# Moving a router's first tiles into the attention before it, with bf16 ranks and marks, three-part weight loads and an earlier normalised input

## The chip, the cores and the metric

One core of one Trainium2 chip runs the whole kernel. The metric is the device time of one execution in microseconds, taken as the median of the runs shown. Engines are PE (TensorE, matmul; PEld is its weight load), DVE (VectorE), ACT (ScalarE), POOL (GpSimd) and SP, which here only issues DMAs.

## The reference

A post-norm vision tower of four blocks on 32 images of 37 tokens, width 256, 1184 tokens in all. The two stages that matter here are the mixture of experts of the third block and the attention stages before and after it.

```python
h = _layernorm(h + _L2_attn_ref(h, ...), axis=-1)
h = _layernorm(h + _L2_ffn_ref(h, ...), axis=-1)
h = _layernorm(h + _L3_attn_ref(h, ...), axis=-1)

def _L2_ffn_ref(x, router_kernel_DE, kernel_gating_EDF, kernel_up_EDF, kernel_down_EFD):
    logits_BSE = jnp.einsum('BSD,DE->BSE', x, router_kernel_DE)          # E = 8
    probs_BSE = jax.nn.softmax(logits_BSE, axis=-1)
    weights_BSK, indices_BSK = jax.lax.top_k(probs_BSE, 2)
    norm_weights_BSK = jax.nn.softmax(weights_BSK, axis=-1)
    ...
    gating = einsum(x, gating_EDF); act = silu(gating); up = einsum(x, up_EDF)
    down = einsum(act * up, down_EFD)                                    # D = 256, F = 512
    out_BSD = jnp.einsum('BSED,BSE->BSD', down, full_weights_BSE)
```

The attention after it starts with a layer norm of its own input (`_L3_attn_ref`: mean, variance, `rsqrt`, then two projections to 128 latents).

## The kernel before

**Tiles.** `X` holds the activations in SBUF as 11 tiles of 111 rows (three images each). Each stage is one block with a program per engine; between stages all semaphores are cleared and all engines meet at a barrier, so a stage starts when the slowest engine of the one before has ended. Each engine works through its own program in order. While a stage runs, SP loads the next stage's weights (`load_next`) into the other of two areas, `weights_even` and `weights_odd`.

**The attention before the experts** (`pair_attention`, stage L2) takes 16 pairs of images in 18 steps `s`. PE's program is written out by hand: in step `s` the scores of pair `s`, the transposes `p_T` of the probabilities of pair `s-1` in two halves, the transposes `o_T` of the output of pair `s-2`, one `o_project` every third step, and the `values` of pair `s-1`. Steps 16 and 17 have no scores any more. Step 16 holds `p_T(15)`, `o_T(14)`, `o_project(4)` and `values(15)`; step 17 holds `o_T(15)`, and then comes `o_project(5)`. DVE adds the residual and takes the statistics, POOL normalises into `X`. Tiles 0 to 7 of `X` are final after unit 3's norm.

**The experts** (`experts_ffn`, stage L2f). A preamble decides where each token goes. PE transposes all 11 tiles of `X` (22 transposes of 128 columns, L1600), ACT copies them to `XT` (L1616), PE multiplies by the 256x8 router (22 fp32 matmuls of 8 columns, L2434). DVE takes the softmax and the two best experts (L2313 to L2342). PE counts, with matmuls by a matrix of ones (L2441 to L2444, 12 matmuls in fp32), how many rows come before each row in each expert. From that DVE works out each row's slot among 27 slots (`NS`) of 128 rows, and builds `tiles`, `marks` (L2376 to L2381) and the one-hot matrices `place` (L2383, two instructions of 11x128 elements), all in fp32. PE multiplies place by marks (L2450, 22 fp32 matmuls of 54 columns): the result names for each slot position its source row and its gate. DVE turns it into `source`, `target` (integers) and `wslot`. One fp32 matmul shows as two records in the trace.

Then comes the loop over 27 slots. POOL gathers 128 rows of `expert_rows` by `source` (L2255, five gathers ahead), PE transposes them (L2459), multiplies by the gate and up weights of the slot's expert (L2464), transposes the product (L2484) and multiplies by the down weights (L2493). DVE scales the result by `wslot` (L2411), and POOL scatters it with an add into `expert_sums` (L2264); each scatter waits for the one before to have landed. SP's queue holds, in this order: `X` to `expert_rows`, the eight experts' weights (one DMA of 1536 KB each, rows of 12 KB, all counted on one semaphore), `X` to `expert_sums`, the next stage's weights, and, behind a wait for the last scatter, `expert_sums` back to `X` in three groups of 4, 4 and 3 tiles.

**The tail.** For each group DVE takes statistics (L1469, L1472), POOL makes `(var + eps) ** -0.5` (L1488, L1490), and DVE alone normalises all 11 tiles (L1480), after the statistics of all groups.

**The attention after the experts** (`latent_attention`, stage L3) starts with statistics of unit 0 (tiles 0 and 1) on DVE (L871), a power and the normalised input `xin` on POOL (L729 to L734), and only then PE's first transposes (L975).

Other stages end in a class `SplitNorm`, which the change uses here too: POOL makes scale and shift per group in three instructions, and both ACT (`on_act`) and DVE (`on_dve`) normalise tiles.

## Time and profile before

| what | value |
|---|---|
| median of 3 runs | 1169.78 us |
| the 3 runs | 1165.82, 1169.78, 1186.6 us |
| the profiled execution | 1169.65 us |
| its span in the trace | 1167.8 us |
| PE, PEld busy | 948.8 us (81%), 725.8 us (62%) |
| DVE, ACT, POOL busy | 584.6 us (50%), 486.1 us (42%), 329.1 us (28%) |
| mean granted clock of PE | 0.868 |
| moved by DMA | 46.53 MB |

The profiled execution lies 0.13 us from the median, and 1.85 us of it lie outside the trace's span. Times inside the trace are counted from the start of the span. A clock of 1.00 is 2.4 GHz and one of 0.50 is 1.2 GHz. The busy shares are means over nine stages.

### The profile page before, as it was taken

What the parts mean: (1) busy time and instruction counts of PE and PEld (TensorE: products, weight loads), DVE (VectorE), ACT (ScalarE), POOL (GpSimd) and SP (SyncE); (2) the same over time, 40 slices, a digit from 0 to 9 for tenths busy, and PEclk for the clock granted to TensorE, in tenths of its full rate; (3) what the DMA queues carried; (4) which work ended last, traced back from release to release, by engine and by line L of the source; (5) the groups of instructions that cost most, each with busy time, mean ns of one, the idle gap of its engine ahead of it and who ended that gap; (6) DMA issues with size and microseconds to landing.
All of it is one profiled execution on the core that took longest, in us unless ns stands there. A gap on an engine that the chain in (4) does not pass through costs nothing. (4 is left out here: it accounts for less than half of the span.)

```text
span 1167.8 us, 25327 instructions
## 1 busy us (share of the span) xinstructions
PE 948.8 (81%) x10056; PEld 725.8 (62%) x10056; DVE 584.6 (50%) x1264; ACT 486.1 (42%) x902; POOL 329.1 (28%) x426
## 2 busy tenths in 40 slices
PE   4899857499999799869975699999178999988564
PEld 4778625377777566658855466666066787777332
DVE  3466756456666289646644122222344456532475
ACT  3345557455555398634430122222013235432354
POOL 0211311534342000021330244443254454531101
PEclk9899968699999898889985699999677999985775
DMA  5200030200000100000009622222310000000001
GB/s 185 100 3 3 3 113 1 76 1 2 0 0 1 43 1 1 0 6 2 3 13 395 239 41 46 46 46 32 62 69 2 3 2 3 3 2 1 1 1 42
DMA packets 20538, 46.53 MB, mean 40 GB/s; under 512 B 4319, under 2 KB 14335, under 8 KB 18766
## 3 DMA queue, kind: packets, MB, share of 16 engines
q1 hardware_dynamic: 15246, 37.93, 9.1%
q0 software_dynamic: 5184, 7.08, 3.9%
q8 instruction: 78, 1.28, 0.5%
q14 instruction: 30, 0.25, 0.1%
HBM read 37.75 MB, written 7.25 MB: 39 GB/s over the span
## 5 line engine op out<-in xcount | busy, mean ns | idle before, releaser
L2464 PE MATMUL psum<-L2f_EW,weights_even 128*128 x216 | 102.8, 600 | 0.4 <-issue 0.4
L2418 DVE TENSOR_TENSOR weights_even<-psum,weights_even 128x512 f32<-128x512 f32 x27 | 18.7, 692 | 109.0 <-PE psum L2464 109.0
L2264 POOL DMA_INDIRECT expert_sums<-weights_even,L2f_target x27 | 42.8, 1584 | 94.1 <-DVE weights_even L2411 91.1
L996 PE MATMUL psum<-L_cT,weights_odd 128*128 128x222 f32 (+1 forms) x192 | 49.0, 389 | 9.2 <-DVE L_by_sin L884 8.0
L2464 PEld LDWEIGHTS psum<-L2f_EW,weights_even 128*128 128x128 f32 x216 | 37.5, 193 | 27.9 <-issue 27.9
L2286 ACT ACTIVATE weights_even<-psum 128x256 f32<-128x256 f32 x27 | 10.4, 384 | 106.8 <-PE psum L2459 74.3
L2152 PE MATMUL psum<-weights_even,L1f_H 128*111 128x256 f32 x176 | 46.7, 424 | 7.5 <-DVE L1f_H L2083 7.5
L2493 PEld LDWEIGHTS psum<-L2f_EW,weights_even 128*128 128x128 f32 x216 | 41.0, 190 | 17.6 <-issue 13.4
L2493 PE MATMUL psum<-L2f_EW,weights_even 128*128 x216 | 51.1, 379 | 0.8 <-ACT weights_even L2291 0.8
L884 DVE TENSOR_TENSOR L_by_cos<-psum,vectors_odd 128x444 f32<-128x444 f32 (+1 forms) x48 | 26.5, 553 | 48.7 <-PE psum L996 48.3
L823 ACT ACTIVATE L_PT<-psum 101x296 f32<-101x296 f32 x32 | 13.3, 417 | 83.2 <-PE psum L1037 82.6
L535 PE MATMUL psum<-L_xT,weights_odd 128*128 128x222 f32 (+1 forms) x192 | 43.9, 379 | 3.3 <-DVE L_V L467 1.9
L395 ACT ACTIVATE L_PT<-psum 101x296 f32<-101x296 f32 x64 | 27.0, 421 | 47.1 <-PE psum L585 47.1
L2152 PEld LDWEIGHTS psum<-weights_even,L1f_H 128*111 128x111 f32 x176 | 34.7, 199 | 18.5 <-DVE L1f_H L2083 8.9
L996 PEld LDWEIGHTS psum<-L_cT,weights_odd 128*128 128x128 f32 x192 | 35.5, 212 | 15.6 <-issue 13.4
L336 POOL TENSOR_TENSOR L_rs<-L_mv,ln_eps 111x2 f32<-111x2 f32 (+1 forms) x12 | 3.0, 254 | 142.9 <-DVE L_mv L482 135.9
L1069 PE MATMUL psum<-weights_odd,L_OT 128*111 128x256 f32 x176 | 41.2, 394 | 0.5 <-ACT L_OT L830 0.5
L2255 POOL DMA_INDIRECT weights_even<-expert_rows,L2f_source x27 | 26.9, 995 | 51.3 <-DVE L2f_source L2402 43.4
L535 PEld LDWEIGHTS psum<-L_xT,weights_odd 128*128 128x128 f32 x192 | 37.0, 213 | 5.2 <-ACT L_xT L364 4.2
L153 PE MATMUL psum<-L1a_W_high,L1a_xT_high 128*111 128x512 f32 x88 | 39.5, 449 | 0.9 <-DVE L1a_xT_low L1298 0.9
L748 POOL TENSOR_TENSOR L_P<-L_P,L_rc 101x592 f32<-101x592 f32 x16 | 19.2, 1200 | 70.5 <-DVE L_rc L902 70.5
L585 PE MATMUL psum<-ident,L_P 101*101 101x101 f32 x256 | 37.1, 268 | 1.8 <-ACT L_PT L395 0.8
(406 smaller groups left out, 2542.2 us busy)
## 6 DMA issues: line engine op xcount, KB each, us to landing
L2f_EW<-experts SPq DMA_DIRECT2D x8, 1536.0 KB, 18.9
weights_even<-L_w SPq DMA_DIRECT2D x4, 1024.0 KB
patch_ring<-patches SPq DMA_DIRECT2D x11, 333.0 KB, 3.3
weights_odd<-L_wqkv SPq DMA_DIRECT2D x2, 768.0 KB
out<-X SPq DMA_DIRECT2D x10, 111.0 KB
expert_rows<-X SPq DMA_DIRECT2D x1, 1056.0 KB, 5.3
expert_sums<-X SPq DMA_DIRECT2D x1, 1056.0 KB, 29.9
weights_odd<-L_wo SPq DMA_DIRECT2D x1, 1024.0 KB
```

The costliest lines, as they stand in the source:

```text
L153: mm = core.nc.tensor.matmul(out, left[a], right[b], start=first and n == 0, stop=last and n == len(passes) - 1)
L395: nc.scalar.activation(PT[:PR, s % 2, 4 * half:4 * half + 4].rearrange("p n (b q) -> p n b q", b=2), cols(core.bank(PTB)[:PR, 0:512], 4, 1 ...
L535: mm = nc.tensor.matmul(bank[:, c * NC2:c * NC2 + n], wqkv[:, kd, first + 128 * c:first + 128 * (c + 1)], xT[:, u % 2, kd, 0:n], start=kd ...
L585: mm = nc.tensor.transpose(core.bank(PTB)[:PR, 128 * i:128 * i + PR], P[:PR, s % 2, 2 * cq:2 * cq + 2].rearrange("p e k -> p (e k)")[:, 0: ...
L884: last = nc.vector.tensor_tensor(dst[:, i % 2, :, 0:k * T].rearrange("p h (i t) -> p h i t", i=k), src, w[table].unsqueeze(1).unsqueeze(1) ...
L996: mm = nc.tensor.matmul(bank[:, h * NC2:h * NC2 + width(u)], wu[:, (2 * g + h) * 128:(2 * g + h + 1) * 128], cT[:, u % 2, n // 4, 0:width( ...
L1069: mm = nc.tensor.matmul(core.bank(M2)[:R, m * D:(m + 1) * D], OT[:, c, first:first + R], wo[:, c, :], start=c == 0, stop=c == 7)
L2152: mm = nc.tensor.matmul(y_bank(t), H[:, c, t * R:(t + 1) * R], w2[:, c, :], start=False, stop=c == nf - 1 and (t % 2 == 1 or t == NT - 1))
L2255: nc.gpsimd.indirect_dma_start(xs[:, j % RING, :], None, rows[:, :], bass.IndirectOffsetOnAxis(ap=source[:, j:j + 1], axis=0)).then_inc(go ...
L2264: nc.gpsimd.indirect_dma_start(sums[:, :], bass.IndirectOffsetOnAxis(ap=target[:, j:j + 1], axis=0), Y[:, j % 2, :], None, compute_op=ALU. ...
L2464: mm = nc.tensor.matmul(core.bank(bank), xsT[:, j % 2, c, :], EW[:, expert[j], first + c * NF:first + (c + 1) * NF], start=c == 0, stop=c ...
L2493: mm = nc.tensor.matmul(core.bank(5)[:, 0:D], HT[:, (j - 1) % 2, c * 128:(c + 1) * 128], EW[:, expert[j - 1], 2 * KD * NF + c * D:2 * KD * ...
```

## The change

- **Router.** The transposes, copies and logits of tiles 0 to 7 (`ROUTED = 8`) move into `pair_attention`: 16 transposes at the start of PE's step 16, 4 ACT copies behind `p_T(15, 1)`, the logits of tiles 0 to 3 at the end of PE's step 16 and those of tiles 4 to 7 at the end of step 17, ahead of `o_project(5)`. The experts' stage keeps tiles 8 to 10.
- **Ranks and marks in bf16.** `ones`, `sooner`, `both`, `place`, `tiles` and `marks` are bf16. The row number goes in two parts that bf16 holds exactly; the gates are no longer in `marks` but go, split in three bf16 parts (`g_parts`, five small DVE instructions ahead of the wait for `mark_ps`), through 22 further matmuls (`gate_marks`) after the sources. `place` is built in four instructions instead of two, `marks` in two instead of four.
- **Weights in three loads.** For each expert, gate, up and down weights are loaded by DMAs of their own (24 of 512 KB, rows of 4 KB), gates of all experts first, with three semaphores. The next stage's weights are issued only after the second slot's result.
- **Tail.** `SplitNorm` with groups of 2, 4 and 5 tiles; ACT normalises tiles 2 to 5, 9 and 10, DVE 0, 1 and 6 to 8. POOL computes one spare power before the tail. A class `Lead` makes the next attention's `xin` of unit 0 there: DVE statistics, POOL power, DVE scaling. `latent_attention` starts with unit 1 on DVE and POOL, and PE transposes unit 0 at once.

```diff
@@ pair_attention
+                    if route and s == NP:
+                        for b in range(ROUTED // 2):
+                            act.wait_ge(rt_ps, b + 1)
+                            bank = core.bank(M1 if b == 3 else S0 + b)
+                            nc.scalar.activation(route.XT[...], bank[...], ACT.Copy).then_inc(rt_done, 1)
...
+                def routed_T():
+                    pe.wait_ge(shifted, NP)
+                    pe.wait_ge(v_done, v_phases(NU, 0))
+                    pe.wait_ge(norm_done, ROUTED // 2)
+                    for b in range(ROUTED // 2):
+                        for m in range(2):
+                            for c in range(KD):
+                                mm = nc.tensor.transpose(bank[...], X[:R, 2 * b + m, c * 128:(c + 1) * 128], core.ident[:R, :R])
+                        mm.then_inc(rt_ps, 1)
+                def routed_logits(first, last):
+                    pe.wait_ge(rt_done, last // 2)
+                    pe.wait_ge(next_sem, 16 * len(next_loads))
+                    for t in range(first, last):
+                        router_logits(core, route.XT, route.router, t)
...
+                    if route and s == NP:
+                        routed_T()
                     if 1 <= s <= NP:
                         p_T(s - 1, 0)
...
                     if 1 <= s <= NP:
                         values(s - 1)
+                    if route and s == NP:
+                        routed_logits(0, ROUTED // 2)
+                if route:
+                    routed_logits(ROUTED // 2, ROUTED)
                 o_project(NU - 1)
@@ experts_ffn, SP
-                for e in range(NEX):
-                    sp.dma_start(EW[:, e, :], core.dram["experts"][e]).then_inc(w_in, 16)
+                for n, sem in enumerate((gates_in, ups_in, downs_in)):
+                    for e in range(NEX):
+                        part = slice(n * KD * NF, (n + 1) * KD * NF)
+                        sp.dma_start(EW[:, e, part], core.dram["experts"][e][:, part]).then_inc(sem, 16)
...
+                sp.wait_ge(y_done, 2)
                 load_next(sp, next_loads, next_sem)
@@ experts_ffn, POOL
-                tail.pool(pool)
+                nc.gpsimd.tensor_tensor(spare[:], core.eps[:], core.nhalf[:, 0:1], ALU.pow)
+                tail.on_pool(pool, 0)
+                pool.wait_ge(lead_var, 1)
+                nc.gpsimd.tensor_tensor(lead.rs[:R], lead.mv[:R, :, 1], core.eps[:R].broadcast_to([R, 2]), ALU.add)
+                pool.drain()
+                nc.gpsimd.tensor_tensor(lead.rs[:R], lead.rs[:R], core.nhalf[:R, 0:2], ALU.pow).then_inc(lead_rstd, 1)
+                tail.on_pool(pool, 1)
+                tail.on_pool(pool, 2)
@@ experts_ffn, ACT
+                tail.on_act(act, 1)
+                tail.on_act(act, 2, 9, 2)
@@ experts_ffn, DVE
-                    V.tensor_tensor(marks[:R, u, :, 0, :], tiles[:R, u], w["row_ids"]..., ALU.mult)
-                    V.tensor_tensor(marks[:R, u, :, 1, :], tiles[:R, u], g2..., ALU.mult)
-                    V.tensor_tensor(place[:R, u], ids..., inside..., ALU.is_equal).then_inc(marked, 1)
+                    V.tensor_tensor(marks[:R, u], tiles[:R, u].unsqueeze(2)..., rows_b[:R].unsqueeze(3)..., ALU.mult)
+                    for p in HALVES:
+                        V.tensor_tensor(place[:R, u, p], ids_b..., inside_b[:R, u, p]..., ALU.is_equal).then_inc(marked, 1)
...
+                V.tensor_copy(g_parts[:R, :, :, 0], g_u)
+                dve.drain()
+                V.tensor_tensor(g_rest[:R, :, :, 0], g_u, g_parts[:R, :, :, 0], ALU.subtract)
...
+                V.tensor_copy(g_parts[:R, :, :, 2], g_rest[:R, :, :, 1])
...
+                for u in range(2):
+                    V.tensor_tensor(gate_marks[:R, u], tiles..., g_parts..., ALU.mult).then_inc(gates_marked, 1)
+                dve.wait_ge(gate_ps, 1)
...
-                for g in range(len(GROUPS)):
+                for g in range(2):
                     dve.wait_ge(back[g], 32)
                     tail.stats(g)
-                for g in range(len(GROUPS)):
-                    tail.norm(dve, g)
+                tail.on_dve(dve, 0)
+                dve.drain()
+                for m in range(2):
+                    V.bn_stats(lead.stat[:R, m], X[:R, m, :])
+                dve.drain()
+                for m in range(2):
+                    last = V.bn_aggr(lead.mv[:R, m], lead.stat[:R, m])
+                last.then_inc(lead_var, 1)
+                dve.wait_ge(back[2], 32)
+                tail.stats(2)
+                dve.wait_ge(lead_rstd, 1)
+                for m in range(2):
+                    V.tensor_scalar(lead.xin[:R, m], X[:R, m, :], lead.mv[:R, m, 0:1], lead.rs[:R, m:m + 1], ALU.subtract, ALU.mult)
+                tail.on_dve(dve, 2, 6, 3)
@@ latent_attention
-                stage(0)
+                stage(1)
                 nc.gpsimd.memset(P[:, :, :, T:64], 0.0).then_inc(zeroed, 1)
-                stage(1)
...
-                input_stats(0)
                 input_stats(1)
...
-                    pe.wait_ge(x_staged, u + 1)
+                    after(pe, x_staged, u)
```

## Rows read from the trace of the kernel before

**Rows 1.** Stretches of one execution: us, each engine's busy time, PE clock, DMA
```profile
607.00:611.00 4.00, 0.00 (x0) 0.00 (x0) 0.79 (x3) 0.00 (x0) 2.79 (x4) 0.50 0.00 0
...
611.10:623.60 12.50, 12.34 (x66) 12.27 (x66) 0.17 (x2) 2.97 (x6) 0.00 (x0) 0.50 0.93 311
...
660.30:821.80 161.50, 159.85 (x594) 97.92 (x594) 31.33 (x54) 41.09 (x82) 62.98 (x48) 0.99 0.26 40
```

**Rows 2.** Timeline, last steps of the attention, PE
```profile
598.62 0.60 PE L585 MATMUL psum<-ident,L_P 101*101 101x101 f32 x4
...
602.11 0.77 PE L598 MATMUL psum<-L_V,L_PT 101*37 101x34 f32 x32
...
604.76 0.39 PE L607 MATMUL psum<-ident,L_O 101*128 101x101 f32 x2 [1.89 <-DVE L_O L455]
...
605.60 1.12 PE L618 MATMUL psum<-weights_odd,L_OT 128*111 128x256 f32 x4 [0.45 <-ACT L_OT L401]
```

**Rows 3.** Timeline, an earlier attention step, four transposes of X
```profile
549.57 0.54 PE L527 MATMUL psum<-ident,X 111*128 111x111 f32 x4
```

**Rows 4.** Timeline, router, ranks and marks in the experts' preamble
```profile
611.12 4.30 PE L1600 MATMUL psum<-ident,X 111*128 111x111 f32 x22 [4.40 <-SPq L126]
...
612.13 0.54 ACT L1616 ACTIVATE weights_even<-psum 128x444 f32<-128x444 f32 x1 [6.58 <-PE psum L1600]
...
615.22 8.25 PE L2434 MATMUL psum<-weights_even 128*111 128x8 f32 x44
...
630.03 3.81 PE L2444 MATMUL psum<-L2f_both,L2f_ones 111*111 111x80 f32 x20
...
638.25 0.84 DVE L2376 TENSOR_TENSOR L2f_slot_tile<-vectors_even,L2f_which 111x297 f32<-111x297 f32 x2
...
640.68 3.15 DVE L2383 TENSOR_TENSOR weights_even<-vectors_even,L2f_inside 111x1408 f32<-111x1408 f32 x2
...
642.35 9.63 PE L2450 MATMUL psum<-L2f_marks,weights_even 111*128 111x54 f32 x44 [8.52 <-DVE weights_even L2383]
...
652.68 0.18 DVE L2402 CAST L2f_source<-L2f_owner 128x27 uint32<-128x27 f32 x1
```

**Rows 5.** Timeline, first gather, first wide work and first scatter of the slots
```profile
653.77 1.30 POOL L2255 DMA_INDIRECT weights_even<-expert_rows,L2f_source  x1 [43.43 <-DVE L2f_source L2402]
...
660.32 0.66 PE L2459 MATMUL psum<-ident,weights_even 128*128 128x128 f32 x2 [8.33 <-DMA weights_even<-expert_rows,L2f_source]
...
671.33 1.89 PE L2493 MATMUL psum<-L2f_EW,weights_even 128*128 x8
...
674.58 1.64 POOL L2264 DMA_INDIRECT expert_sums<-weights_even,L2f_target  x1 [13.24 <-DVE weights_even L2411]
```

**Rows 6.** Issues of the experts' weights, then DMA totals of 627:640 and 652:656
```profile
612.18 8.42 SPq L2239 DMA_DIRECT2D L2f_EW<-experts  x8
...
DMA packets 510, 5.55 MB, mean 427 GB/s; under 512 B 59, under 2 KB 59, under 8 KB 59
...
DMA packets 440, 1.48 MB, mean 370 GB/s; under 512 B 44, under 2 KB 105, under 8 KB 429
```

**Rows 7.** Timeline, experts' tail and start of the next attention
```profile
827.66 2.75 SPq L2246 DMA_DIRECT2D X<-expert_sums  x6
...
831.97 1.41 DVE L1469 BATCH_NORM_STATS2 L2f_stat<-X 111x6 f32<-111x256 f32 x4 [9.75 <-DMA X<-expert_sums]
...
838.70 1.05 POOL L1490 TENSOR_TENSOR L2f_rs<-L2f_rs,minus_half 111x4 f32<-111x4 f32 x1 [4.58 <-issue]
...
839.78 3.80 DVE L1480 TENSOR_SCALAR X<-X,L2f_mv,L2f_rs 111x256 f32<-111x256 f32 x11 [2.00 <-POOL L2f_rs L1490]
...
849.54 0.97 PE L975 MATMUL psum<-ident,L_xin 111*128 111x111 f32 x4 [27.84 <-POOL L_xin L734]
```

**Rows 8.** Timeline, bf16 transposes in the last stage, PE at half clock
```profile
1100.64 0.93 PE L2678 MATMUL psum<-identb,L3f_XQ 111*128 111x111 bf16 x8 [3.23 <-DVE L3f_XQ L2581]
```

**Rows 9.** A stretch of the next attention
```profile
880.00:893.60 13.60, 12.87 (x185) 9.93 (x185) 6.01 (x10) 3.12 (x6) 8.53 (x13) 0.50 0.01 3
```

More of the change, by code:

```diff
@@ L1497, with router_logits, __init__ @@
 AHEAD, AHEAD_L3 = 8, 10
+ROUTED = 8
+LOGITS = 3
+def router_logits(core, XT, router, t):
+    for c in range(KD):
+        mm = core.nc.tensor.matmul(core.bank(LOGITS)[:R, t * 8:(t + 1) * 8], XT[:, c, t * R:(t + 1) * R], router[:, c, :],
+                                   start=c == 0, stop=c == KD - 1)
+    return mm
+class Route:
+    def __init__(self, core, w):
+        self.router = cols(w["L2_router"], KD, 8)
+        self.XT = cols(core.areas[0][:, KD * 8:KD * 8 + KD * TOK], KD, TOK)
+class Lead:
+    def __init__(self, stack, core):
+        sb = lambda n, s, d=F32: stack.enter_context(core.nc.sbuf_tensor(f"lead_{n}", s, d))
+        self.xin = cols(core.areas[0][:, 5888:6400], 2, D)
+        self.stat, self.mv, self.rs = sb("stat", [128, 2, 6]), sb("mv", [128, 2, 2]), sb("rs", [128, 2])
 class Int8Weights:
@@ L2203, in experts_ffn @@
         Y = cols(area[:, at + 6 * NF:at + 6 * NF + 2 * D], 2, D)
[L2204 to L2206 removed]
+        assert at + 6 * NF + 2 * D + KD * NEX <= 5888
+        tiles = sb("slot_tile", [128, 2, NT, NS], BF16)
+        marks, gate_marks = sb("marks", [128, 2, NT, 2, NS], BF16), sb("gate_marks", [128, 2, NT, 3, NS], BF16)
+        ones, sooner = sb("ones", [128, R], BF16), sb("sooner", [128, R], BF16)
+        ids_b, rows_b = sb("ids_b", [128, 128], BF16), sb("rows_b", [128, NT, 2], BF16)
+        which_b, inside_b = sb("which_b", [128, 2, NT], BF16), sb("inside_b", [128, 2, NT], BF16)
+        g_parts, g_rest = sb("g_parts", [128, 2, NT, 3], BF16), sb("g_rest", [128, 2, NT, 2])
+        spare = sb("spare", [128, 1])
         lg, pr = sb("logits", [128, NT, NEX]), sb("probs", [128, NT, NEX])
@@ new lines, in _ @@
+                for u in range(2):
+                    V.tensor_tensor(gate_marks[:R, u], tiles[:R, u].unsqueeze(2).broadcast_to([R, NT, 3, NS]),
+                                    g_parts[:R, u].unsqueeze(3).broadcast_to([R, NT, 3, NS]), ALU.mult).then_inc(gates_marked, 1)
+                dve.wait_ge(gate_ps, 1)
+                found = core.bank(5)[:, 0:3 * NS]
+                V.tensor_copy(wslot[:], found[:, 0:NS])
+                for p in range(1, 3):
+                    dve.drain()
+                    V.tensor_tensor(wslot[:], wslot[:], found[:, p * NS:(p + 1) * NS], ALU.add)
@@ L2441, in _ @@
                 nc.tensor.matmul(core.bank(2)[:R, 0:NT * NEX], ones[:R, :R], flat, start=True, stop=True)
-                nc.tensor.matmul(core.bank(1)[:R, 0:NT * NEX], w["sooner"], flat, start=True, stop=False)
+                nc.tensor.matmul(core.bank(1)[:R, 0:NT * NEX], sooner[:R], flat, start=True, stop=False)
                 for d in range(1, NT):
@@ L2755, in tower @@
         run[2](2)
-    for n in range(3, 7):
+    prepared["route"] = Route(core, w[6])
+    for n in range(3, 6):
         run[n](n)
     with ExitStack() as stack:
+        prepared["lead"] = Lead(stack, core)
+        run[6](6)
         prepared["glu"] = GluWeights(stack, nc, w[8])
```

142 lines of the change are left out of this document (89 added, 53 removed).

## The prediction

> **What bounds the kernel now.** I read the stretches first, then the timeline of the stages that the diff touches. The stretches show three kinds of time around the experts. In the loop over the slots PE is busy 159.9 of 161.5 us at full clock [rows 1]; the diff changes nothing there, so the loop's length stays. Ahead of it lies a preamble of 49.2 us, from PE's first transpose at 611.12 to the first slot's transpose at 660.32 [rows 4, 5], in which PE and DVE take turns and PE runs at 0.50: it fell there by 607, behind the attention's thin end, and 12.5 us of transposes and 8-column matmuls did not raise it [rows 1]. Behind it lies a tail of DMA, POOL and DVE in which PE waits 27.84 us [rows 7]. The change shortens preamble and tail and pays in the attention. The sum is therefore made of the chain of single events, not of busy shares.
>
> **The attention's end.** Three pieces go into PE's in-order program. (a) 16 transposes stand ahead of p_T(15), which began at 598.62, just when its input was there. Four such transposes took 0.54 us at full clock, the last one's end included [rows 3], so about 0.11 each: 1.8 us, with the waits ahead of them long met; I take 2.0, which moves every later step. (b) The logits of tiles 0 to 3, 8 matmuls. All 22 took 8.25 us at half clock [rows 4], 0.375 each, so 3.0 us at half and 1.5 at full clock. They stand behind values(15), which ended at 602.88; PE then waited 1.89 us for DVE [rows 2]. At full clock they fit into that wait and cost nothing; the copies they need (0.54 us each [rows 4]) are ready, since ACT has nothing else there but two o_T and p_T copies, and o_project(4) gives it 2 us. At half clock they cost 1.1. (c) The logits of tiles 4 to 7 stand between o_T(15) and o_project(5), where PE had 0.45 us to spare [rows 2]: 1.5 - 0.45 = 1.05 at full clock, 2.55 at half. Which clock? It had fallen by 607, in the thin stretch behind values(15) [rows 1, 2]. Everything there moves by 2.0, and I let the fall move with it, to 609, when (c) is done; so I take full clock and add 0.25 for a slower o_project(5). Sum **+3.3 us**; ends +2.8 and +6.8 (all at half clock, with 1.12 us of o_project doubled). POOL and DVE have no new work here.
>
> **The preamble.** All prices are at half clock, which also ruled there before.
> - Router: 3 tiles are left. PE ended the logits at 623.47. Now 4 transposes (4.30 / 22 = 0.195 each [rows 4], 0.8), a copy (0.54 and some 0.3 of waits) and 6 matmuls of 0.375 (2.25) end at 3.9 us behind the start instead of 12.35. **-8.45**. DVE's new casts hide behind this.
> - Ranks: 12 fp32 matmuls; ten of them took 3.81 us, so 4.6. The nearest bf16 row at half clock is 8 transposes in 0.93, 0.116 each [rows 8]: 1.4. **-3.2**; ends -3.6 (0.08 each) and -1.8 (0.23 each, one fp32 record).
> - Marks: before, PE started its 22 matmuls at 642.35 and ended at 651.98, 8.15 us behind DVE's last place instruction at 643.83; source was written at 652.86 [rows 4]. In bf16 DVE writes the same elements; two more instructions for place and two fewer for marks cancel, and one more cast adds 0.1. DVE's instruction rate stays (the same operation took 1.575 us for 1408 elements [rows 4]); PE's 22 matmuls by 0.116 run beside it, and the last five end at about 644.7. But DVE's program is now the bound: expert ids (1.35), then five small instructions for the gates at an estimated 0.25 each, drain included, then three for the source: 643.9 + 1.35 + 1.25 + 0.7 = 647.2. **-5.65**; if bf16 halved DVE's element time, for which no row speaks, 2.7 more would go. The gates' own 22 matmuls and DVE's products of 891 elements (about 1 us each) take some 4.5 us after that, hidden by the first gather's 6.5 us. Cover gone, they cost up to 1 us.
>
> On DVE, the Trainium skill (VectorE: DVE Perf Modes) says that a two-source operation gets its double rate if every tensor is 16-bit with step 1 or -1; here the second source is broadcast with step 0, so no gain. No row here shows such an operation. With the double rate the result would be 1148.3.
>
> - First gather: it took 6.5 us from issue to PE's transpose, with the queues full of weights [rows 5]. The queues are full in the new place too, so I keep 6.5. It would be at worst the whole backlog, at best 3 us less.
>
> So the first slot starts 17.3 us sooner after the stage's start: 49.2 becomes 31.9.
>
> **The weights.** 12.58 MB in rows of 4 KB instead of 12. With 12 KB rows the queue moved 427 GB/s, with mostly 4 KB rows 370 [rows 6]. By 12.5 us, 3.9 MB had moved, 1.25 of it expert_rows [rows 1]; with the rest and 0.65 MB of gathers 10.6 MB remain, 28.6 us at 370: down weights at 41.1 us behind the start. The first matmul by them, at 671.33 before [rows 5], now stands at 42.9. It fits, by 1.8 us; gates and ups, each a third, come well before their use. expert_sums (1.25 MB) is written by 45, the first scatter (674.58 before) needs it at 46.1. SP issues 24 instead of 8 (8.42 us [rows 6], so up to 25): it stays ahead of the data. Cost **0**; at 311 GB/s [rows 1] 3.7 us of stall. The next stage's 2.9 MB now wait for y_done 2 and move beside the first slots: nothing stands behind them in SP's queue before the last scatter, gathers are five slots ahead, and a scatter may be late by some 5 us before DVE's second buffer waits. Cost 0.
>
> The Trainium skill speaks against the split: DMA: Bandwidth & Descriptors, section Bandwidth, asks for at least 1 MiB per DMA and gives 341 GB/s at 1 MB; these have 0.5 MB. At that rate the down weights stall PE for about 0.7 us, 1151.7 in all. No row here has loads of that size alone.
>
> **The tail.** Before: loads issued at 827.66, statistics from 831.97, POOL's power only at 838.70 behind 4.58 us in which it waited for nothing shown, DVE's 11 tiles from 839.78 to 843.58 [rows 7]. Now the spare power takes that pause while the loads fly. Two tiles are in at 830.9; DVE's statistics end at 832.2; POOL's scale of two at 833.8 (estimated 1.5); DVE's next four at 835.2, its two tiles and the lead's statistics at 837.1; the lead's power at 838.3; POOL's groups of four and five at 840.3 and 842.5 (2.0 and 2.2: power 1.05 [rows 7], two small ones, two drains); the last tiles on ACT and DVE at 843.8. So the stage ends 0.2 later, and POOL, not DVE, sets it. But PE now starts the next attention by transposing, instead of at 849.54, 5 us behind that stage's start at 844.5: **-4.7** with the 0.2. Unit 1's statistics and scaling on DVE and POOL lie beside unit 0's projections. Ends -6 and -1.7.
>
> **Sum.** 1169.65 + 3.3 - 8.45 - 3.2 - 5.65 - 4.7 = 1150.95, with the 1.85 us outside the span unchanged. The median is 0.13 above the profiled time: **1151**, 1.6% faster. Its own range is 1147 to 1156.
>
> **Rivals.**
> 1. *Weights bound the start.* At 311 GB/s the down weights come 3.7 us late: 1155. For it: the slack is 1.8 us of 42.9. Against: 370 was measured with small packets among them. 0.16.
> 2. *The spare power doesn't take the pause*, the change not doing what it says: the 4.58 us come again behind the loads, of which about 3 reach the end: 1154. For it: no row says what the pause is. 0.08.
> 3. *The attention's end at half clock*, +6.8: 1154.5. For it: 12.5 us of such transposes and logits left the clock at 0.50 [rows 1], so they may not hold it at 1.00 either. 0.10.
> 4. *The next attention keeps its clock.* It ran at 0.50 for 13.6 us with PE busy 12.9 [rows 9]. Nothing in the change aims at that, but everything there moves by 19 us; if it stays at 1.00, some 5.5 us fall away: 1145.5. The opposite, a new fall elsewhere, is as possible and costs the same: 1156.5. 0.14 and 0.06.
> 5. *Slower than before.* If DMAs of 4 KB rows fall below 216 GB/s, the 10.6 MB take over 49 us and PE's stall exceeds the 18.7 us gained; at 200 GB/s it is 22.6: 1174. Against: every stretch with weights moved 311 or more. 0.03.
>
> **Chances.** Forecast 0.43, the rest as given. 2% is about what a measurement of this kernel tells from no change; it lies at 1146.4. Rival 4's better half (0.14) and the far lower edge of the forecast (0.06) lie below: 0.2. Slower by over 2%: 0.01. Within: 0.79. The range of 8 in 10 is 1143 to 1160.
>
> **What will show it.** In the new trace: p_T(15) 2 us behind values(14), o_project(5) about 3 us later than before; lg_ps 4 us behind the stage's start; ten and more bf16 matmuls at about 0.12 us in ranks and marks; first slot 32 us behind the start; no DMA wait at the first down matmul; POOL's power in the tail without a pause; PE in the next attention within 1 us of its start. Wrong would make it a gather that waits for the whole backlog, a clock different from the one before in the attention's end or the slots' first steps, or a longer POOL chain in the tail.

## The result, and the profile after

| what | before | after |
|---|---|---|
| median | 1170.28 us (4 runs, 1165.82 to 1186.6) | 1149.6 us (4 runs, 1145.2 to 1154.38) |
| the profiled execution, its span | 1169.65, 1167.8 us | 1149.84, 1148.0 us |
| mean granted clock of PE | 0.868 | 0.874 |

The ratio is 0.9845, 95% interval 0.9811 to 0.9878: 1.5% faster, and within the 2% that a measurement of this kernel tells from no change. Some executions of the same kernel run about 2% longer at a lower granted clock; the ratios leave them out (the medians don't), and of the two profiles further on that are of such executions, those with eight loads and with paced loads, only the stretches at the experts are read.

The whole span is no good ruler for terms of 2 us, so I cut it at single events of PE's program. The chain that the change touches runs from the start of values(14), the last work ahead of the moved transposes, to PE's first transpose in the next attention: 252.10 us before (597.44 to 849.54), 235.36 after (596.62 to 831.98), 16.74 less. The span fell by 19.80; 3.06 of that lie outside of the chain.

| piece of the chain, us | before | after | difference | forecast |
|---|---|---|---|---|
| values(14) to p_T(15) | 1.18 | 2.56 | +1.38 | +2.0 |
| p_T(15) to the stage's start (SP's first issue) | 12.54 | 14.77 | +2.23 | +1.3 |
| start to logits done | 12.42 | 4.08 | -8.34 | -8.45 |
| `both` written to the ranks read | 4.74 | 1.37 | -3.37 | -3.2 |
| ranks read to the instruction that writes `source` | 18.81 | 13.04 | -5.77 | -5.65 |
| softmax and top two, and `source` to PE's first slot transpose | 13.19 | 13.56 | +0.37 | 0 |
| that transpose to the last scatter | 163.52 | 163.46 | -0.06 | 0 |
| last scatter to the next attention's first transpose | 25.70 | 22.52 | -3.18 | -4.7 |
| sum | 252.10 | 235.36 | -16.74 | -18.7 |

Each piece runs between the starts of two instructions; only the one of `both` begins where its writing ends.

The attention's end, PE's timeline (start, length, line, output and inputs, tile, count, idle time before it and its releaser) and one ACT row, to be held against [rows 2]:

```profile
597.60 1.74 PE L638 MATMUL psum<-ident,X 111*128 111x111 f32 x16
599.18 0.52 PE L593 MATMUL psum<-ident,L_P 101*101 101x101 f32 x4
...
601.22 1.83 ACT L430 ACTIVATE weights_even<-psum 128x444 f32<-128x444 f32 x4
602.53 0.77 PE L606 MATMUL psum<-L_V,L_PT 101*37 101x34 f32 x32
...
603.23 1.73 PE L1536 MATMUL psum<-weights_even 128*111 128x8 f32 x16
...
605.19 0.39 PE L615 MATMUL psum<-ident,L_O 101*128 101x101 f32 x2 [0.23 <-DVE L_O L463]
605.42 2.19 PE L1536 MATMUL psum<-weights_even 128*111 128x8 f32 x16
...
607.47 2.03 PE L626 MATMUL psum<-weights_odd,L_OT 128*111 128x256 f32 x4
```

Two stretches of the same place (length, then busy time of PE, PEld, DVE, ACT and POOL, and behind them the granted clock, DMA share and GB/s):

```profile
606.00:607.00 1.00, 1.00 (x9) 1.00 (x8) 0.00 (x0) 0.00 (x0) 1.00 (x1) 0.67 0.00 0
607.00:608.00 1.00, 1.00 (x5) 0.89 (x5) 0.00 (x0) 0.00 (x0) 1.00 (x2) 0.50 0.00 0
```

The first eight logits matmuls (16 records) fill the pause ahead of o_T(15), which shrank from 1.89 to 0.23 and comes 6.01 behind p_T(15) where it came 6.14 behind it: they cost nothing. The second eight push o_project(5) from 6.98 to 8.29 behind p_T(15), and the clock falls to 0.50 while they run (0.67 on average in the first of the two stretches), so that o_project(5) takes 2.03 instead of 1.12.

The preamble, the answer to [rows 4, 5] (PE, DVE and POOL rows of its timeline):

```profile
613.98 1.34 PE L2554 MATMUL psum<-ident,X 111*128 111x111 f32 x6 [4.49 <-PEq L126]
615.59 2.41 PE L1536 MATMUL psum<-weights_even 128*111 128x8 f32 x12 [0.26 <-ACT weights_even L2355]
...
623.84 1.07 PE L2567 MATMUL psum<-L2f_both,L2f_ones 111*111 111x80 bf16 x10
...
629.60 0.85 DVE L2464 TENSOR_TENSOR L2f_slot_tile<-L2f_ids_b,L2f_which_b 111x297 bf16<-111x297 bf16 x2
...
631.22 1.69 DVE L2472 TENSOR_TENSOR weights_even<-L2f_ids_b,L2f_inside_b 111x768 bf16<-111x768 bf16 x2
...
635.25 0.41 PE L2574 MATMUL psum<-L2f_marks,weights_even 111*128 111x54 bf16 x5 [0.28 <-DVE weights_even L2472]
...
637.99 0.18 DVE L2501 TENSOR_SCALAR L2f_source<-L2f_mark 128x27 uint32<-128x27 f32 x1
...
639.09 1.66 POOL L2323 DMA_INDIRECT weights_even<-expert_rows,L2f_source  x1 [25.97 <-DVE L2f_source L2501]
...
639.63 1.93 PE L2580 MATMUL psum<-L2f_gate_marks,weights_even 111*128 111x81 bf16 x22 [3.97 <-DVE L2f_gate_marks L2506]
...
646.00 0.66 PE L2589 MATMUL psum<-ident,weights_even 128*128 128x128 f32 x2 [4.43 <-DMA weights_even<-expert_rows,L2f_source]
...
656.98 1.89 PE L2627 MATMUL psum<-L2f_EW,weights_even 128*128 x8
```

The marks' matmuls end 2.3 us ahead of `source`: DVE's own order is the bound. The gates' 22 matmuls are over at 641.56, while the first gather is still under way: PE waits 4.43 us for it. The first down matmul has no wait. Two stretches show DMA with loads of 0.5 MB:

```profile
626.00:640.00 14.00, 2.09 (x28) 1.51 (x29) 12.01 (x38) 0.00 (x0) 0.91 (x1) 0.50 1.03 412
640.00:650.00 10.00, 4.79 (x27) 2.61 (x25) 1.12 (x4) 2.05 (x3) 5.50 (x6) 0.50 1.03 398
```

The tail, which answers to [rows 7]:

```profile
809.46 1.55 POOL L2332 DMA_INDIRECT expert_sums<-weights_even,L2f_target  x1 [2.95 <-DMA expert_sums<-weights_even,L2f_target]
810.46 1.16 POOL L2341 TENSOR_TENSOR L2f_spare<-ln_eps,minus_half 128x1 f32<-128x1 f32 x1
813.18 2.75 SPq L2314 DMA_DIRECT2D X<-expert_sums  x6
...
817.36 0.19 POOL L1743 TENSOR_TENSOR L2f_rs<-L2f_mv,ln_eps 111x2 f32<-111x2 f32 x1 [5.74 <-DVE L2f_minus_mean L1736]
...
822.13 0.70 POOL L1745 TENSOR_TENSOR L2f_rs<-L2f_rs,minus_half 111x2 f32<-111x2 f32 x1 [4.58 <-issue]
...
823.21 0.74 DVE L1763 TENSOR_SCALAR X<-X,L2f_mv,L2f_rs 111x256 f32<-111x256 f32 x2 [2.02 <-POOL L2f_norm_shift L1747]
...
827.93 3.06 ACT L1755 ACTIVATE X<-X,L2f_norm_shift,L2f_rs 111x256 f32<-111x256 f32 x6 [22.71 <-POOL L2f_norm_shift L1747]
...
831.93 0.35 SPq L131 DMA_DIRECT2D weights_even<-L_wg  x1
...
831.98 0.97 PE L1005 MATMUL psum<-ident,weights_even 111*128 111x111 f32 x4 [24.62 <-PEq L126]
```

The spare power ran at once, and the pause of 4.58 us, to the hundredth the one of [rows 7], stands again between POOL's first small addition and its first power. Between these two instructions the program has one thing: the first `pool.drain()` since the indirect DMAs.

### The profile page after: what moved, and what is told of

Same layout as the page of the kernel before. It is cut to its first block and busy times, and to the rows that moved or that the text cites. A ratio compares the mean times of both kernels' runs of the same rounds, so it can differ in the third digit from the quotient of the medians.

```text
span 1148.0 us, 25356 instructions
## 1 busy us (share of the span) xinstructions
PE 932.5 (81%) x10044; PEld 709.3 (62%) x10044; DVE 587.7 (51%) x1275; ACT 488.4 (43%) x908; POOL 328.0 (29%) x428
## 5 line engine op out<-in xcount | busy, mean ns | idle before, releaser
L2526 DVE TENSOR_TENSOR weights_even<-psum,weights_even 128x512 f32<-128x512 f32 x27 | 18.7, 691 | 105.7 <-PE psum L2594 105.7
L543 PE MATMUL psum<-L_xT,weights_odd 128*128 128x222 f32 (+1 forms) x192 | 41.0, 361 | 3.3 <-DVE L_V L475 1.9
L2193 PE MATMUL psum<-L1f_XT,weights_even 128*128 128x333 f32 (+1 forms) x128 | 37.7, 441 | 1.1 <-ACT L1f_XT L2034 0.7
```

Of the source, the lines that this page charges most:

```text
L543: mm = nc.tensor.matmul(bank[:, c * NC2:c * NC2 + n], wqkv[:, kd, first + 128 * c:first + 128 * (c + 1)], xT[:, u % 2, kd, 0:n], start=kd ...
L2193: mm = nc.tensor.matmul(core.bank(bank)[:, 0:k * R], w1[:, kk, c * 128:(c + 1) * 128], XT[:, kk, group_cols(t0, k)], start=kk == 0, stop=k ...
```

## The experiments

All start from the changed kernel. Besides the time, each is read by the chain (235.36 in the changed kernel) and by its pieces.

**The ruler first.** The changed kernel itself once more, without any edit.

> The changed kernel itself once more, unchanged, beside the version with both repairs on the same chip. Expected: 1149 to 1153 us, ratio to before 0.982 to 0.988, and by segments p_T(15) to stage start 14.8, start to first slot 32.0, last scatter to the next first transpose 22.5, each within 0.3; what stands outside of these (the time up to p_T(15), and from the next first transpose to the end) differs from the first profile by up to 3 us, which would show how much of a total is not the change's. Rival: these segments themselves vary by a microsecond or more, and then single profiles don't bear the differences read from them.

Measured: 1151.71 us (1145.86 to 1172.48, 6 runs), ratio 0.9858 (0.9817 to 0.99). Chain 235.27, and its pieces 2.57, 14.90, 32.01 and 22.42: within 0.13 of the first profile. Outside of it stood 908.7 us of 1144.0 instead of 912.6 of 1148.0. So the chain repeated to 0.1 us in these two profiles, while the rest of the program differed by 3.9 us between two profiles of one kernel. That is the size of the 3.06 us above, and no cause in the change is needed for them. Two is few, though: in the seven further kernels that leave the tail alone, the piece from the last scatter to the next first transpose is 22.56 to 22.97, and the first gather takes 6.7 to 7.2 us in those that leave it alone. So a difference below half a microsecond in one piece is not read as an effect. The ratios can't order the versions at all: the one without the lead has 0.9832, although its chain is 3.6 us longer.

**The pause in the tail.** One kernel adds a drain behind the spare power, the other has the drain in its place.

```diff
                 nc.gpsimd.tensor_tensor(spare[:], core.eps[:], core.nhalf[:, 0:1], ALU.pow)   # left out in the second
+                pool.drain()
                 tail.on_pool(pool, 0)
```

> The changed kernel with a drain on POOL behind the spare power. In the changed kernel's trace the 4.58 us pause of POOL stands in the tail as before, between the first add of the first group (ends at 817.55) and its power (822.13), although the spare power ran at 810.46 in 1.16 us. Between add and power stands the first drain after the scatters. Theory A, the pause belongs to the first drain after a run of indirect DMAs: it now falls behind the spare power, some 811.6 to 816.2, beside the loads, the power of the first group stands 0.34 us behind its add, and the tail shortens by about 2.0 us, by the 2.02 us that DVE waited for the first scale. From the last scatter's issue to PE's first transpose of the next attention: 20.5 us instead of 22.5. Theory B, the pause comes with the first statistics-dependent work whatever was drained before: it stays at 4.6 us at the same place, 22.5 us.

> The changed kernel with a drain in place of the spare power. Theory A (the pause is the first drain's): as with both, pause hidden, about 20.5 us from the last scatter to the next attention's first transpose; the spare power is worth nothing, and the first group's power takes about 0.7 us without it. Theory C (the power needs a first call to be fast): the first group's power or the wait ahead of it is 0.5 us or more longer than with the spare power.

Measured, with both: 1154.66 us (4 runs, 1144.67 to 1168.34), ratio 0.9857 (0.9676 to 1.0038), which tells nothing. Drain alone: one run, 1148.92. The chains tell: 233.46 and 232.92, with 20.62 and 20.16 from the last scatter to the next first transpose instead of 22.52. The drain alone, POOL and DVE in the tail:

```profile
811.22 1.55 POOL L2332 DMA_INDIRECT expert_sums<-weights_even,L2f_target  x1 [2.88 <-DMA expert_sums<-weights_even,L2f_target]
819.14 0.20 POOL L1743 TENSOR_TENSOR L2f_rs<-L2f_mv,ln_eps 111x2 f32<-111x2 f32 x1 [6.37 <-DVE L2f_minus_mean L1736]
819.49 0.72 POOL L1745 TENSOR_TENSOR L2f_rs<-L2f_rs,minus_half 111x2 f32<-111x2 f32 x1 [0.15 <-issue]
...
822.63 0.73 DVE L1763 TENSOR_SCALAR X<-X,L2f_mv,L2f_rs 111x256 f32<-111x256 f32 x2
```

The power now follows the addition after 0.15 us of pause. So the 4.58 us belong to the first drain in this stage, not to the first power. Put behind the last scatter, it lies beside the scatter's landing and the loads. It was worth 2.36 us, not 4.58, because DVE works on beside the pause: it takes the second group's statistics and only then stands 2.02 us for the first scale (823.21 in the changed kernel). With the drain moved it has no wait there (822.63 above). The spare power is worth nothing.

Is it only that this drain is a stage's first, or the first after a long time? A stage without indirect DMAs, the changed kernel's earlier feed-forward L1f, answers this. Its first drain comes 88 us after POOL's last work and stands between these two rows, with 0.14 us between them:

```profile
480.03 0.37 POOL L1743 TENSOR_TENSOR L1f_rs<-L1f_mv,ln_eps 111x6 f32<-111x6 f32 x1 [88.33 <-DVE L1f_minus_mean L1736]
480.54 1.63 POOL L1745 TENSOR_TENSOR L1f_rs<-L1f_rs,minus_half 111x6 f32<-111x6 f32 x1
```

So it isn't every stage's first drain; that it is the time alone is unlikely, though in the experts' stage POOL's last drain lay longer back, some 206 us. What else is different is the run of 54 indirect DMAs ahead of it. No run varies these, so that they are the reason stays inferred. It isn't a wait for the last scatter to land: that had landed by 813.18, when SP, which waits for it, issued the loads, and the pause begins at 817.55.

**Logits 4 to 7 behind o_project(5).** The transposes stay where they are.

```diff
-                if route:
-                    routed_logits(ROUTED // 2, ROUTED)
                 o_project(NU - 1)
+                if route:
+                    routed_logits(ROUTED // 2, ROUTED)
```

> The changed kernel with the logits of tiles 4 to 7 behind o_project(5) instead of ahead of it. In the changed kernel they took 2.19 us there, o_project(5) began at 607.47 instead of about 606.0, and took 2.03 us with the clock at 0.50 instead of 1.12. Theory A, they cost because they stand in the chain: behind o_project(5) PE waits some 4.4 us for DVE, POOL and the barrier, so they are hidden even at half clock (3 us); the stage's end comes 1.4 us sooner, 2.3 if o_project(5) also runs at full clock. From p_T(15) to the experts' first transpose: 12.5 to 13.4 us instead of 14.8. Theory B, the last logits end after the POOL norm and delay the barrier: less than 1 us gained.

Measured: 1153.03 us (1148.21 to 1157.29), ratio 0.9866 (0.9767 to 0.9965); p_T(15) to the stage's start 12.98 instead of 14.77; chain 234.49.

```profile
607.75 1.67 PE L626 MATMUL psum<-weights_odd,L_OT 128*111 128x256 f32 x4 [0.45 <-ACT L_OT L403]
609.22 3.02 PE L1536 MATMUL psum<-weights_even 128*111 128x8 f32 x16
613.90 1.35 PE L2554 MATMUL psum<-ident,X 111*128 111x111 f32 x6 [1.67 <-PEq L126]
```

The eight logits matmuls (3.02 us at half clock) lie beside DVE's and POOL's work on the last unit, PE is idle for another 1.67, and the logits are done 4.09 behind the start as before. What is left over 12.54 is the clock: it fell at 608.2, inside o_project(5). (The chain got shorter by only 0.87 of the 1.79 us, since the first scatter came 0.87 later behind the stage's start, 47.15 instead of 46.28; why stays open.)

**All of it in the gaps.** Transposes behind values(15), ACT's copies behind its copy for o_T(15), all logits behind o_project(5).

```diff
-                    if route and s == NP:
+                    if route and s == NP + 1:          # ACT: the four copies
...
-                    if route and s == NP:
-                        routed_T()
                     if 1 <= s <= NP:
                         p_T(s - 1, 0)
...
                     if route and s == NP:
-                        routed_logits(0, ROUTED // 2)
+                        routed_T()
+                o_project(NU - 1)
                 if route:
+                    routed_logits(0, ROUTED // 2)
                     routed_logits(ROUTED // 2, ROUTED)
-                o_project(NU - 1)
```

> The changed kernel with all of its moved router work in the attention's gaps: the 16 transposes behind values(15) instead of ahead of p_T(15), ACT's four copies behind its copy for o_T(15), all 16 logits matmuls behind o_project(5). Theory A, PE has 1.9 us to spare ahead of o_T(15) and the whole norm of the last unit behind o_project(5), so the move costs nothing: p_T(15) to stage start 14.77 becomes 12.4 to 12.9 (12.54 before the change), and what stood ahead of p_T(15) goes too, 1.4 us (seen as values(14) to p_T(15)); logits done 4.08 behind the stage's start as now. Rival B, the logits come too late there, behind ACT's copies and at half clock, and the stage's end waits for them: 14 us or more, or logits done later than 4.5 behind the start.

Measured: 1149.65 us (1146.72 to 1151.38), ratio 0.9805 (0.9753 to 0.9857); values(14) to p_T(15) 1.18, p_T(15) to start 12.56, logits done 4.08 behind the start; chain 232.13.

```profile
602.37 1.74 PE L638 MATMUL psum<-ident,X 111*128 111x111 f32 x16
...
604.33 0.39 PE L615 MATMUL psum<-ident,L_O 101*128 101x101 f32 x2 [0.22 <-DVE L_O L463]
...
605.00 1.85 ACT L430 ACTIVATE weights_even<-psum 128x444 f32<-128x444 f32 x4
605.16 1.12 PE L626 MATMUL psum<-weights_odd,L_OT 128*111 128x256 f32 x4 [0.45 <-ACT L_OT L403]
606.12 3.20 PE L1535 MATMUL psum<-weights_even 128*111 128x8 f32 x32
```

Eight tiles' router work costs the attention nothing at all (12.54 and 1.18 before). The clock was still 1.00 at 609.00 and fell at 610.0, 13.0 us behind values(14), with the same instructions in another order. (The chain is 3.23 us shorter, against 3.59 in these two pieces.)

**The router back.** All eleven tiles in the experts' stage (`ROUTED = 0`, nothing in the attention).

> The changed kernel with all 11 tiles' transposes, copies and logits in the experts' stage again. Theory A, the move is worth what the two traces show: start to logits done 4.08 becomes 12.4, the attention's end (p_T(15) to stage start) 14.77 becomes 12.5, p_T(15) comes 1.4 to 2.0 us earlier; net 4.3 to 5 us later at the first slot. The weights, counted from the stage's start, come 8 us sooner relative to the first slot. Rival B, what follows the logits had been waiting for weights or for the queue: start to first slot grows by less than 6 us and the net is below 2 us.

Measured: 1159.5 us (1158.62 to 1163.14), ratio 0.9904 (0.9869 to 0.9938); p_T(15) to start 12.56, start to logits 12.42, values(14) to p_T(15) 1.18; chain 241.55. The first slot comes 4.55 later behind values(14). So the move is worth 8.34 gross and 4.6 net. The chain grew by 6.2, since the slots and the tail took 1.6 us longer; that part stays open.

**fp32 again.** `both`, `ones`, `sooner`, `tiles`, `marks`, `place` and `gate_marks` in fp32, with the small tensors that DVE makes them from, same instructions.

```diff
-        tiles = sb("slot_tile", [128, 2, NT, NS], BF16)
+        tiles = sb("slot_tile", [128, 2, NT, NS])          # and the others alike
```

> The changed kernel with both, ones, sooner, tiles, marks, place and gate_marks in fp32 again, all loops and instruction counts as changed (the same values, exactly held). Theory A, fp32 matmuls on PE were the price: ranks (both written to need read) 1.37 becomes 4.7; tiles written to source written 8.39 becomes 13.5 to 14.5, since PE's 22 fp32 matmuls of 54 columns bound it again; then 22 fp32 matmuls of 81 columns stand ahead of PE's first slot transpose and no longer hide behind the first gather, so that gather to first transpose becomes 12 to 15 instead of 6.91. First slot 14 to 17 us later, no other segment changed. Rival B, the gain came from DVE's shorter order of instructions and its 16-bit outputs: ranks as in A, but tiles to source stays below 11, and place and marks on DVE take longer than 1.69 and 0.78 us for the same instructions.

Measured: 1158.93 us (1155.34 to 1161.53), ratio 0.9897 (0.9855 to 0.9938); ranks 4.74, `tiles` to `source` 12.82 instead of 8.39, gather to first transpose 10.02 instead of 6.91; chain 246.07.

```profile
634.04 0.85 DVE L2464 TENSOR_TENSOR L2f_slot_tile<-L2f_ids_b,L2f_which_b 111x297 f32<-111x297 f32 x2
...
635.66 1.69 DVE L2472 TENSOR_TENSOR weights_even<-L2f_ids_b,L2f_inside_b 111x768 f32<-111x768 f32 x2
636.67 9.63 PE L2574 MATMUL psum<-L2f_marks,weights_even 111*128 111x54 f32 x44 [7.31 <-DVE weights_even L2472]
...
646.34 0.18 DVE L2497 TENSOR_SCALAR L2f_empty<-psum 128x27 f32<-128x27 f32 x1 [4.31 <-PE psum L2574]
...
648.50 9.67 PE L2580 MATMUL psum<-L2f_gate_marks,weights_even 111*128 111x81 f32 x44 [2.19 <-DVE L2f_gate_marks L2506]
```

DVE's instructions for `tiles` and place take 0.85 and 1.69 us in fp32 as in bf16: the gain is all PE's. The 22 marks matmuls take 9.63 where DVE now waits 4.31 for them. The forecast for this kernel was a microsecond too high, because place in four instructions lets PE start earlier than before the change (2.6 us behind `tiles`, before 4.1). The gates' matmuls, at the same clock of 0.50, cost 9.67 for 81 columns, as much as the marks' for 54. So they stick out of the gather's cover by 3.1 us instead of 5 to 8, and the first slot comes 10.9 later, not 14.

**The weights in one wait.** Eight loads of 1536 KB, and PE's first slot waits for all.

```diff
-                for n, sem in enumerate((gates_in, ups_in, downs_in)):
-                    for e in range(NEX):
-                        part = slice(n * KD * NF, (n + 1) * KD * NF)
-                        sp.dma_start(EW[:, e, part], core.dram["experts"][e][:, part]).then_inc(sem, 16)
+                for e in range(NEX):
+                    sp.dma_start(EW[:, e, :], core.dram["experts"][e]).then_inc(gates_in, 16)
...
-                            pe.wait_ge(ups_in, 16 * NEX)
...
-                            pe.wait_ge(downs_in, 16 * NEX)
```

> The changed kernel with the experts' weights again in one DMA of 1536 KB per expert, all counted on one semaphore that the first slot waits for. Theory A, the three loads let the first slots start on the gate weights: in the changed kernel the queue had moved some 13.4 MB by 36 us behind the stage's start and the last weights land at about 37.6, the first wide matmul is at 34.1; with one wait PE stands 2 to 4 us at the first slot, and the time rises by as much, ratio to the kernel before about 0.987. Theory B, rows of 12 KB and DMAs of 1.5 MB move faster than rows of 4 KB and 0.5 MB, by 427 to 370: all weights are in by 33 to 34 us and nothing is lost, ratio as for the changed kernel, 0.985 or below.

Measured: 1161.56 us (1152.34 to 1184.04, 10 runs), ratio 0.9923 (0.9876 to 0.9969); PE's first slot transpose to its first wide matmul 9.52 instead of 2.06.

```profile
666.61 0.69 PE L2587 MATMUL psum<-ident,weights_even 128*128 128x128 f32 x2 [1.03 <-DMA weights_even<-expert_rows,L2f_source]
674.43 1.22 PE L2592 MATMUL psum<-L2f_EW,weights_even 128*128 x1 [7.14 <-DMA L2f_EW<-experts]
```

The weights were complete 41.9 us behind the stage's start (632.55 to 674.43), and the first wide matmul was due at 34.4: the shortened preamble runs into them by 7.5 us. The direction is theory A's, its size was put too low. The three-part order takes that stall away whole. (The chain is 244.40, 9.0 us longer; some 1.5 beyond the wait are not explained.)

**Holding the down loads back** until the first gather has landed.

```diff
                 for n, sem in enumerate((gates_in, ups_in, downs_in)):
+                    if n == 2:
+                        sp.wait_ge(got0, 16)
```

> The changed kernel with SP waiting for the landing of the first gather before it issues the eight down loads (4.2 MB) and expert_sums. Theory A, the first gather is slow because it shares the DMA engines with the backlog: gather to first transpose 6.91 becomes 4.5 to 5.5, the first slot comes 1.5 to 2.4 us sooner, and the down weights, issued from about 30 us behind the start, land at 40.5 to 42 and stall the first down matmul (at 41 then) by 0 to 1 us. Rival B, the gather takes 6.5 to 7 us whatever is queued: first slot unchanged, and the first down matmul waits 0 to 2 us for the DMA; the time is the same or up to 2 us longer.

Measured: 1156.83 us (1154.46 to 1158.75), ratio 0.9889 (0.9853 to 0.9925); gather to first transpose 4.00, start to first slot 29.16, but first transpose to last scatter 168.76 instead of 163.46; chain 238.24.

```profile
642.19 1.48 PE L2591 MATMUL psum<-ident,weights_even 128*128 128x128 f32 x4 [1.52 <-DMA weights_even<-expert_rows,L2f_source]
...
658.32 1.99 PE L2629 MATMUL psum<-L2f_EW,weights_even 128*128 x8 [3.67 <-DMA L2f_EW<-experts]
```

2.9 us of the gather's 6.9 are the backlog. But from 638 to 642, around the end of the hold, DMA had only 220 GB/s, the down weights landed 45.3 us behind the start (40.5 to 42 had been expected), and what was won came back as a wait of 3.67 (0 to 1 expected) and slower first slots.

**At most three loads under way.** The last four ups loads and all down loads are each issued when the one three before it has landed, on four semaphores in turn, for which PE waits.

```diff
+                        i = NEX * (n - 1) + e
+                        sem = paced[i % 4] if n else gates_in
+                        if i >= 4:
+                            sp.wait_ge(paced[(i - 3) % 4], 16 * ((i - 3) // 4 + 1))
```

> The changed kernel with its 24 loads in the same order, but from the fifth ups load on SP issues a load only when the one three before it has landed, so that at most three (1.5 MB) are under way, and expert_sums follows the last. Theory A, the first gather's time is the backlog ahead of it, and a short backlog keeps the DMA engines busy all the same: gather to first transpose 6.91 becomes 4.5 to 5.9 (4.00 was seen with an empty queue), the first slot comes 1.0 to 2.4 us sooner, the down weights land at 41 to 43 behind the start and the first down matmul, due at 41 to 42, waits under 1.5 us: first scatter 0.5 to 2 us sooner behind the start than 46.28. Rival B, three loads under way don't fill the engines: the rate between 20 and 36 us behind the start falls below 350 GB/s, the down weights land after 44 and the first scatter is later than 46.3.

Measured: 1154.52 us (1150.45 to 1176.66), ratio 0.9848 (0.9798 to 0.9898); gather to first transpose 6.02, first scatter 51.37 behind the start instead of 46.28; chain 240.70.

```profile
660.00:666.00 6.00, 1.87 (x22) 1.49 (x22) 2.60 (x6) 0.00 (x0) 4.50 (x4) 0.50 0.93 319
...
681.91 3.53 PE L2634 MATMUL psum<-L2f_EW,weights_even 128*128 x8 [3.51 <-DMA L2f_EW<-experts]
```

Rival B: 1.5 MB under way move 319 GB/s (318 to 356 in the stretches around it) where a full queue moved 398 or more, and the weights come last again. Theory A fell, in this form; the gather gained 0.9 us and PE waited 3.5.

**No lead.** The next attention makes statistics, power and `xin` of unit 0 itself.

> The changed kernel without the lead: the next attention takes statistics, power and xin of unit 0 itself, as before. Theory A, the lead is worth about as predicted: the tail loses DVE's 1.8 us and POOL's 0.9 us of lead work, of which about 1 us shows, and PE's first transpose comes 5.0 us behind the stage's start instead of 0; last scatter to that transpose 22.5 becomes 26 to 27, and the next attention's first scores come 3 to 5 us later behind the last scatter. Rival B, the lead only moves the work: the first scores come within 1 us of the changed kernel's, since unit 1's input and POOL's combine bound them.

Measured: 1155.33 us (1150.55 to 1179.21), ratio 0.9832 (0.9788 to 0.9876); last scatter to first transpose 26.30 instead of 22.52; chain 238.93.

```profile
832.22 0.75 DVE L903 BATCH_NORM_STATS2 L_pstat<-X 111x6 f32<-111x256 f32 x2 [1.02 <-PEq L126]
...
837.18 0.97 PE L1007 MATMUL psum<-ident,weights_even 111*128 111x111 f32 x4 [28.22 <-POOL weights_even L766]
```

The lead takes 5.0 us off the attention's start and puts 1.2 into the tail (stage end 22.47 behind the last scatter with it, 21.30 without). Later, at PE's first matmuls for `c_nat`, the latents of the keys and values (L1041 at 849.30 in the changed kernel, L1043 at 854.49 here), the distance is still 3.8 us, 39.8 and 43.6 behind the last scatter: the gain is kept, and rival B fell.

**Both repairs.** All router work in the gaps, and the drain in place of the spare power.

> The two repairs together: all of the moved router work in the attention's gaps, and a drain in place of POOL's spare power. Theory A, both add up: p_T(15) to stage start 12.5, last scatter to the next attention's first transpose 20.2 to 20.6, everything else as in the changed kernel; 5.5 to 6 us less than the changed kernel in the same chain, so some 1144 us and a ratio to before of 0.976 to 0.980. Rival B, a gain in one place is given back at the other or in the next attention (a clock that falls elsewhere, a barrier that another engine reaches last): less than 3 us against the changed kernel.

Measured: 1146.52 us (1143.05 to 1167.07, 6 runs), ratio 0.9845 (0.9788 to 0.9902), beside the changed kernel's 1151.71 and 0.9858 on the same chip: by the times the two can't be told apart. By the chain they can: 229.46 against 235.27, with 12.56 and 20.10 where theory A said 12.5 and 20.2 to 20.6. The repairs add up to 5.8 us. The ratio expected, 0.976 to 0.980, did not come.

## Why the prediction was right, point by point

1151 was forecast and 1149.6 measured. Most terms were right in mechanism and size, but that the sum agrees to 1.4 us is in part luck: 2.0 us too much gain was claimed in the chain, rival 2 (chance 0.08) came true in the tail, and against both stand 3.06 us that came from outside of the chain, where two profiles of one kernel differ as much.

- **The attention's end, +3.3: +3.6.** (a) 2.0 was 1.38: the 16 transposes took 1.74 and let p_T(15) come that much later only. (b) was hidden as said. (c) 1.05 was 1.31. The term that was off is the 0.25 for a slower o_project(5): it was 0.91. The step behind it, "I let the fall move with it, to 609", failed: the clock fell 9.7 us behind values(14) as it had before (9.6), under PE's logits. The first row of [rows 1] shows only that it had fallen; where, and what it does when work is added, the forecast had assumed. Rival 3 (all at half clock) was wrong for (a) and (b), and right for the last 1.2 us (0.26 of (c) and 0.91 of o_project(5)).
- **Router, -8.45: -8.34; ranks, -3.2: -3.37; marks, -5.65: -5.77.** The experiments with the router back and with fp32 give 8.34 and 3.37 back. That DVE's program would bound the marks, with bf16 no faster on it, held to 0.1 us. The Trainium skill (VectorE: DVE Perf Modes) wants every tensor of a two-source operation 16-bit and with step 1 or -1 for its double rate; with a broadcast second source the trace agrees that there is no gain: 0.85 and 1.69 us in both types.
- **First gather, 0: +0.36.** That is within what this piece differs between kernels that don't touch it (6.7 to 7.2). It waits for part of the backlog, as the kept 6.5 said; the 3 us "at best" are real (2.9), but two ways of taking them cost more in the weights.
- **Weights, 0: 0.** 41.1 forecast for the down weights; all weights were complete at 41.9 in the kernel with eight loads, and in the changed one the wait at 43.0 was met. Rival 1 (311 GB/s) and rival 5 (216) did not come: 398 to 412 with loads of 0.5 MB. The Trainium skill (DMA: Bandwidth & Descriptors, section Bandwidth) asks for at least 1 MiB per DMA and gives 341 GB/s at 1 MB, measured with DMAs issued from GpSimd. Here SP issues, into a queue kept full, and the trace differs: 0.5 MB loads moved at 398 to 412, and PE's waits show no cost of the split.
- **The tail, -4.7: -3.18.** The step that failed is "Now the spare power takes that pause while the loads fly". The pause belongs to the first drain, not to the power, so rival 2 came true: 4.58 us between the first addition and its power, as before. Its price, 3 us, was too high: DVE's statistics of the second group went on beside the pause, and 2.4 is what the repaired version gives back. That the stage would end only 0.2 later failed with it (22.47 behind the last scatter instead of 20.68; 20.12 with the drain alone); the 5 us at the next attention's start came as forecast (4.97).
- **Rival 4.** The next attention kept its pattern: the clock falls 30.5 us behind its first transpose before and 30.4 after. No gain, no loss.

## What to carry to other kernels

When a cover is meant to take a pause, first find which instruction owns the pause: here it was the drain, one line away from the power that the trace names. Work moved into an in-order engine is free only in its gaps: put into one pause and behind the last step that others wait for, the same 48 records cost nothing, ahead of steps that others wait for 3.6 us. And when a preamble is shortened (here from 49 to 32 us), the loads that used to be early become the bound (7.5 us), so they are to be split by order of use.

## What the runs showed of the hardware

- The first drain of POOL behind a run of indirect DMAs stopped it for 4.58 us, the same in both kernels, although the last one had been issued 6.5 us earlier (8.7 before the change) and had landed; directly behind the last scatter it cost nothing that showed. A first drain in a stage without indirect DMAs left 0.14. That the indirect DMAs are the reason is inferred.
- Loads of 0.5 MB moved at 398 to 412 GB/s in a full queue, and at 318 to 356 with three under way. An indirect gather issued into the full queue took 6.9 us to its use, and 4.0 into one that ran empty a microsecond later.
- The clock fell 9.6 to 9.8 us behind values(14) whether PE was idle there (before), in logits (after) or in o_project(5) (logits last); with all the transposes and logits behind values(15) it fell only after 13.0 us. What decides that I haven't settled.
